# Row sums of an attention kernel: pair tiles joined by adding transfers, straight turns, another tile order

## The reference

```
xn  = layernorm(x)
x  += attention(xn) + experts(xn)
# attention, for each batch entry and head:
S   = q @ k.T * 32 ** -0.5            # 2048 x 2048
P   = exp(S - max(S)) / sum(exp(S - max(S)))
out = (P @ v) @ proj_w.T + proj_b
```

## Time and profile before

| | us |
|---|---|
| profiled execution | 5082.81 |
| its span on the core | 5081.0 |
| median of three runs | 5081.68 |
| TensorE busy | 4905.3 (97%) |
| TensorE weight loads | 2978.3 (59%) |
| VectorE busy | 3225.3 (63%) |
| ScalarE busy | 2454.4 (48%) |
| GpSimd busy | 3283.1 (65%) |
| mean granted TensorE clock | 0.983 of full speed |

### The profile page before, as it was taken

One profiled execution on the slowest core, in us unless ns is written; L12 is line 12 of the kernel. 1 busy time (PEld: TensorE's weight loads), 2 busy tenths in 40 slices (PEclk: granted clock), 3 DMA queues, 4 the chain that ended last, 5 costly groups with the idle time before them and its releaser, 6 DMA issues. The chain is left out here.

```text
span 5081.0 us, 84542 instructions
## 1 busy us (share of the span) xinstructions
PE 4905.3 (97%) x25932; PEld 2978.3 (59%) x25932; DVE 3225.3 (63%) x5424; ACT 2454.4 (48%) x4653; POOL 3283.1 (65%) x925
## 2 busy tenths in 40 slices
PE   8999999999899999999999999999999999999979
PEld 6878878878555555545554554555455455555447
DVE  4232333232577877777777777777777777778624
ACT  2121121121166666656665666666566566666631
POOL 1212211211288888888888888888888888888830
PEclk9999999999799999999999999999999999999989
DMA  5352433433311111211211211211211111121056
GB/s 171 93 156 87 131 112 117 123 116 118 89 30 49 46 41 48 47 43 43 51 37 43 57 35 44 53 41 39 53 46 35 49 48 41 41 53 30 14 177 236
DMA packets 217465, 366.39 MB, mean 72 GB/s; under 512 B 41156, under 2 KB 74948, under 8 KB 208840
## 3 DMA queue, kind: packets, MB, share of 16 engines
q1 hardware_dynamic: 217032, 360.85, 25.5%
HBM read 224.96 MB, written 134.74 MB: 71 GB/s over the span
## 5 line engine op out<-in xcount | busy, mean ns | idle before, releaser
L848 POOL TENSOR_TENSOR p_pair<-p_sb 128x2048 f32<-128x2048 f32 x512 | 2338.0, 4588 | 523.2 <-PE mx_ps L998 442.7
L903 DVE TENSOR_REDUCE unit_max<-mx_ps 128x1 f32<-128x512 f32 x4096 | 2512.0, 681 | 217.7 <-PE mx_ps L978 210.3
L889 ACT ACTIVATE p_sb<-st_ps 128x512 f32<-128x512 f32 x4096 | 2110.4, 616 | 1083.6 <-PE st_ps L1044 1074.3
L978 PE MATMUL mx_ps<-k_x,q_x 96*128 96x512 f32 x4096 | 1700.1, 419 | 71.8 <-DVE unit_max L903 52.1
L1044 PE MATMUL st_ps<-q_x,k_x 97*128 97x512 f32 x4096 | 1626.5, 410 | 19.5 <-issue 16.8
L978 PEld LDWEIGHTS mx_ps<-k_x,q_x 96*128 96x128 f32 x4096 | 784.1, 192 | 619.6 <-DVE unit_max L903 256.4
L990 PE MATMUL o_ps<-p_sb,v_sb 128*32 128x512 f32 x8192 | 996.9, 605 | 5.1 <-ACT p_sb L889 5.1
L1044 PEld LDWEIGHTS st_ps<-q_x,k_x 97*128 97x128 f32 x4096 | 774.6, 189 | 352.9 <-ACT p_sb L889 151.3
L285 POOL TENSOR_TENSOR h_lo<-h_f,h_hi 128x512 fp32r<-128x512 f32 x128 | 165.4, 1293 | 691.6 <-DVE h_hi L469 691.6
L838 POOL TENSOR_TENSOR p_pair<-p_pair 128x2048 f32<-128x2048 f32 x128 | 586.9, 4585 | 10.0
L990 PEld LDWEIGHTS o_ps<-p_sb,v_sb 128*32 128x32 f32 x8192 | 214.9, 109 | 504.0 <-ACT p_sb L889 298.7
(11 more groups left out here) (93 smaller groups left out, 3755.8 us busy)
## 6 DMA issues: line engine op xcount, KB each, us to landing
q_x<-q_hi_d SPq DMA_DIRECT2D x128, 256.0 KB, 7.2
k_x<-k_hi_d SPq DMA_DIRECT2D x68, 256.0 KB, 4.1
xt<-x SPq DMA_DIRECT2D x64, 256.0 KB, 2.7
stage<-w SPq DMA_DIRECT2D x32, 512.0 KB, 5.1
q_hi_d<-qk_hi SPq DMA_DIRECT2D x64, 256.0 KB, 3.0
q_lo_d<-qk_lo SPq DMA_DIRECT2D x64, 256.0 KB, 3.8
k_hi_d<-qk_hi SPq DMA_DIRECT2D x64, 256.0 KB, 2.6
k_lo_d<-qk_lo SPq DMA_DIRECT2D x64, 256.0 KB, 3.3
```

Source lines behind the costliest of these rows:

```text
L848: pool.tensor_tensor(p_pair[:, slot, :, :], p_sb[:, 2 * i % SLOTS, :, :], p_sb[:, (2 * i + 1) % SLOTS, :, :], ALU.add).then_inc(pair_done, 1)
L889: act.activation(p_sb[:, kt % SLOTS, h, :], st_ps[bank(g, m)][:, :], ACT.Exp, scale=SCALE).then_inc(exp_done, 1)
L903: dve.reduce_max(unit_max[:, n // 4, n % 4:n % 4 + 1], mx_ps[UNIT_PLACE[n] % RING][:, :], AX.X).then_inc(bank_read, 1)
L978: pe.matmul(mx_ps[UNIT_PLACE[n] % RING][:, :], q_x[qc][0:R, h, t * P:(t + 1) * P], k_x[u][0:R, h, kc * 512:(kc + 1) * 512], start=True, st ...
```

## The change

- Each pair's two tiles are added by GpSimd as before, but into four p_pair slots whose roles a, b, c, d rotate from group to group (pair_slots). Four times a group GpSimd issues an adding transfer (join): a whole 1 MB pair slot is added to another inside SBUF. One more add on GpSimd joins the last pair. So GpSimd does 9 adds a group instead of 10.
- There are three row-sum parts instead of six: slot a after two joins (in step 7), slot d after four joins (in step 2 of the next group), slot a again after GpSimd's last add (in step 3 of the next group). Slot a holds pairs 0, 1 and 2 at first; d holds pairs 3, 4 and 5; and a holds 6 and 7 at the end.
- p_sb has 7 slots instead of 8, filled by the tile's number in the whole run modulo 7.
- All turns are straight code on all engines.
- The order of tiles in the steps is another; T stands behind V alone, and a wait for its bank is added. A group has 68 places.

```diff
-    SLOTS = 8
+    SLOTS = 7
-    ADDS = [(0, 0, -1), (1, 1, -3), ("four", 1, None), (2, 0, None), (3, 2, -2), ("four", 2, None),
-            (4, 0, None), (5, 1, 0), (6, 2, 1), (7, 0, 2)]
-    PARTS = [(3, 1, 4), (6, 2, 6), (7, 0, 7), (8, 1, 7), (9, 2, 8), (10, 0, 9)]
+    def pair_slots(group):
+        a, b, c, d = 0, 1, 2, 3
+        for _ in range(group):
+            a, b, c, d = c, b, d, a
+        return a, b, c, d
+    NA, NJ = NP + 1, 4
+    PARTS = [(2, 0, False, 7), (4, 0, True, 10), (0, NA, False, 11)]
...
-        p_pair = sb("p_pair", [P, 3, 4, TOK], F32)
+        p_pair = sb("p_pair", [P, 4, 4, TOK], F32)
...
-        STEPS = ["SUSSUVZUSUSUSUSUSU", "SUSSUVZUSUSUSUSUSU", "SUSSUVUSUSUSUSUSU", "SUSSUVUSUSUSUSUSU",
-                 "SUSSUVZUSUSUSUSUSU", "SUSSUVUSUSUSUSUSU", "SUSSUVZTUSUSUSUSUSU", "SUSSUVZUSUSUSUSUSU"]
+        STEPS = ["USUSUSUVUSSUSUSUS", "USUSUSUVUSSUSUSUS", "USUSUSUVZUSSUSUSUS", "USUSUSUVZUSSUSUSUS",
+                 "USUSUSUVUSSUSUSUS", "USUSUSUVUSSUSUSUS", "USUSUSUVTUSSUSUSUS", "USUSUSUVZUSSUSUSUS"]
...
-                with sp.Fori(1, TURNS - 1) as L:
+                for L in range(1, TURNS - 1):
...
+                def join(into, slot):
+                    pool.dma_start(p_pair[:, into, :, :], p_pair[:, slot, :, :], accum_op=ALU.add).then_inc(joined, 16)
+                def group(at):
+                    a, b, c, d = pair_slots(at)
+                    if at > 0:
+                        pool.wait_ge(joined, at * NJ * 16)
+                    pair(at, 0, a)
+                    pool.wait_ge(pair_done, at * NA)
+                    pair(at, 1, b)
+                    pool.wait_ge(pair_done, at * NA + 2)
+                    join(a, b)
+                    if at > 0:
+                        pool.wait_ge(sum_done, at * NS - 1)
+                    pair(at, 2, c)
+                    if at > 0:
+                        pool.wait_ge(sum_done, at * NS)
+                    pair(at, 3, d)
+                    pool.wait_ge(pair_done, at * NA + 3)
+                    pool.wait_ge(joined, (at * NJ + 1) * 16)
+                    join(a, c)
+                    pair(at, 4, b)
+                    pool.wait_ge(pair_done, at * NA + 5)
+                    pool.wait_ge(joined, (at * NJ + 2) * 16)
+                    join(d, b)
+                    pair(at, 5, c)
+                    pool.wait_ge(sum_done, at * NS + 1)
+                    pair(at, 6, a)
+                    pool.wait_ge(pair_done, at * NA + 6)
+                    pool.wait_ge(joined, (at * NJ + 3) * 16)
+                    join(d, c)
+                    if at > 0:
+                        normalise(at)
+                    pair(at, 7, b)
+                    pool.wait_ge(pair_done, at * NA + NP)
+                    pool.tensor_tensor(p_pair[:, a, :, :], p_pair[:, a, :, :], p_pair[:, b, :, :], ALU.add).then_inc(pair_done, 1)
...
-                                act.activation(p_sb[:, kt % SLOTS, h, :], st_ps[bank(g, m)][:, :], ACT.Exp,
+                                act.activation(p_sb[:, (L * G * KT + n) % SLOTS, h, :], st_ps[bank(g, m)][:, :], ACT.Exp,
...
-                    adds, slot, at = PARTS[i]
-                    pe.wait_ge(pair_done, L * G * NA + g * NA + adds)
+                    joins, adds, in_d, at = PARTS[i]
+                    slot = pair_slots(L * G + g)[3 if in_d else 0]
+                    if joins:
+                        pe.wait_ge(joined, ((L * G + g) * NJ + joins) * 16)
+                    else:
+                        pe.wait_ge(pair_done, (L * G + g) * NA + adds)
...
                         elif step == "T":
+                            emptied(0, -1, TURNED, True, False)
                             turn_rows(1)
```

More of the change, by code:

```diff
@@ L590, in attention_stage @@
     RING = 4
-    ADDS = [(0, 0, -1), (1, 1, -3), ("four", 1, None), (2, 0, None), (3, 2, -2), ("four", 2, None),
-            (4, 0, None), (5, 1, 0), (6, 2, 1), (7, 0, 2)]
-    PARTS = [(3, 1, 4), (6, 2, 6), (7, 0, 7), (8, 1, 7), (9, 2, 8), (10, 0, 9)]
-    PAIR_ADDED = [[pair for pair, _, _ in ADDS].index(i) + 1 for i in range(NP)]
-    NA, NS = len(ADDS), len(PARTS)
-    NORM = 9
+    def pair_slots(group):
[5 more added lines that the diff above has]
+    PARTS = [(2, 0, False, 7), (4, 0, True, 10), (0, NA, False, 11)]
+    NS = len(PARTS)
     ctx = ExitStack()
@@ L645, in attention_stage @@
         SK = 4 * KT
[L650 to L651 removed]
+        STEPS = ["USUSUSUVUSSUSUSUS", "USUSUSUVUSSUSUSUS", "USUSUSUVZUSSUSUSUS", "USUSUSUVZUSSUSUSUS",
+                 "USUSUSUVUSSUSUSUS", "USUSUSUVUSSUSUSUS", "USUSUSUVTUSSUSUSUS", "USUSUSUVZUSSUSUSUS"]
         FIRST = sum(s.count("U") for s in STEPS[AHEAD:])
+        PARTS_AT = [at for _, _, _, at in PARTS]
         FILLS = [(j, i, step) for j in range(NP) for i, step in enumerate(STEPS[j]) if step in "UTZ"]
@@ L665, in filled @@
                 return not (last and g + (2 if j >= AHEAD else 1) >= G) and (g > -2 or j >= AHEAD)
-            return step == "Z" and not (first and (g < 0 or g == 0 and j < 2))
+            return step == "Z" and not (first and (g < 0 or g == 0 and j + NP in PARTS_AT))
         def reads(g, place, first, last):
@@ L688, in attention_stage @@
         PART_PLACE = {at: PLACE[at % NP, STEPS[at % NP].index("Z")] for at in PARTS_AT}
-        PARTS_ON = {at: sum(at == x for _, _, x in PARTS) for at in PARTS_AT}
-        PARTS_BY = {at: sum(x <= at for _, _, x in PARTS) for at in PARTS_AT}
+        PARTS_BY = {at: n + 1 for n, at in enumerate(PARTS_AT)}
         ALL_READS = read_count(TURNS - 1, G - 1, PLACES, False, True)
@@ L828, in normalise @@
                     pool.tensor_tensor(o_inv[:, :], o_raw[:, :], o_inv[:, :], ALU.mult).then_inc(o_done, 1)
[L830 to L849, removed]
@@ L851, in _, with pair @@
-                turn(0, True)
-                with pool.Fori(1, TURNS) as L:
-                    turn(L, False)
+                def pair(at, i, slot):
+                    pool.wait_ge(exp_done, at * SK + 8 * i + 8)
+                    n = at * KT + 2 * i
+                    pool.tensor_tensor(p_pair[:, slot, :, :], p_sb[:, n % SLOTS, :, :], p_sb[:, (n + 1) % SLOTS, :, :],
+                                       ALU.add).then_inc(pair_done, 1)
+                def join(into, slot):
+                    pool.dma_start(p_pair[:, into, :, :], p_pair[:, slot, :, :], accum_op=ALU.add).then_inc(joined, 16)
@@ L854, in _ @@
+                for at in range(NQ * QC):
+                    group(at)
                 normalise(NQ * QC)
@@ L887, in turn @@
                                     old = n - SLOTS
-                                    act.wait_ge(pair_done, since(L * G * NA, old // KT * NA + PAIR_ADDED[old % KT // 2]))
-                                act.activation(p_sb[:, kt % SLOTS, h, :], st_ps[bank(g, m)][:, :], ACT.Exp,
+                                    act.wait_ge(pair_done, since(L * G * NA, old // KT * NA + old % KT // 2 + 1))
+                                act.activation(p_sb[:, (L * G * KT + n) % SLOTS, h, :], st_ps[bank(g, m)][:, :], ACT.Exp,
                                                scale=SCALE).then_inc(exp_done, 1)
                 turn(0, True, False)
-                with act.Fori(1, TURNS - 1) as L:
+                for L in range(1, TURNS - 1):
                     turn(L, False, False)
@@ L958, in _ @@
                 turn(0, True, False)
-                with dve.Fori(1, TURNS - 1) as L:
+                for L in range(1, TURNS - 1):
                     turn(L, False, False)
@@ L1068, in sum_parts @@
                                 pe.wait_ge(shift_done, L * G + G)
-                            for i, (_, _, at) in enumerate(PARTS):
+                            for i, (_, _, _, at) in enumerate(PARTS):
                                 if at == (j if mine else j + NP):
@@ L1083, in turn @@
                                 elif not (last and g == G - 1):
+                                    emptied(L, g, TURNED, first, last)
                                     turn_rows(L * G + g + 2)
                 turn(0, True, False)
-                with pe.Fori(1, TURNS - 1) as L:
+                for L in range(1, TURNS - 1):
                     turn(L, False, False)
@@ L1093, in _ @@
                 for i in range(NS):
-                    if PARTS[i][2] >= NP:
-                        sums(TURNS - 1, G - 1, i, PART_PLACE[PARTS[i][2]])
+                    if PARTS[i][3] >= NP:
+                        sums(TURNS - 1, G - 1, i, PART_PLACE[PARTS[i][3]])
 def output_stage(nc, proj_wT, o_d, y_d, out):
```

7 lines of the change are left out of this document (3 added, 4 removed).

## The result

The changed kernel takes 4842.35 us (median of 4 runs, 4836.55 to 4845.29) against 5081.59: ratio 0.9526, interval 0.951 to 0.9543. The profiled execution took 4836.55 us, its span is 4834.7. The forecast was 4875.

A forecast was written before the change was run, and what follows sets the result against it. TensorE's own work (97% busy) was taken as the bound, GpSimd 6 us from it. From 5082.8 us, 62 x (54.52 - 51.1) = 212 off and 4.6 on for the tail gave 4875 us; own range 4820 to 4945 (0.49).

The forecast's parts named there:

- Straight turns: Attention stage's 48 looped intervals: written straight they take 53.26 us each, 79 us off in all.
- Places: Ring of four banks: 68 places instead of 70 padded to 72 remove TensorE's 0.95 us wait before step 0.
- Parts: TensorE's row sums: three parts a group fewer, 0.87 us each, 2.6 us off.
- i: GpSimd's time to issue one adding transfer: 1.1 us taken, ends 0.43 and 1.72.
- l: Adding transfer's time from issue to landing: 7.9 us (2.5 fixed, two reads of 2.7), ends 5.2 and 10.6.
- The path over pair 6: Step 7's part, pair 6, join 4's issue, multiply, copy, exponential, step 0's seventh score: TensorE stands 1.1 us a group.
- GpSimd's own sum: GpSimd per group: 42.6 us work, four issues of 1.1, 3.3 landing wait, 0.4 gaps: 50.7 us.
- two loops that meet once a group seldom mesh: TensorE's and GpSimd's cycles both come out near 50.8 us a group, so 51.1 us is taken.
- A: Rival, GpSimd's waits on landings: joins land late, GpSimd is the bound; slower, 5199 us, up to 5353; chance 0.22.
- C: Rival, GpSimd's issues: dearer joins at 1.72 us each, still faster, 5006 us; chance 0.20 together with the late-small-DMA rival.
- B: Rival, GpSimd's joins: cheap issues (0.43 us), quick landings (5.2 us), 4790 us; chance 0.07 for below 4820.
- D: Rival: a small DMA late, 1 to 3 us a group, 4937 to 5061 us; chance 0.20 together with dearer joins.

## Why the prediction was right, point by point

- **Straight turns**: 79 us forecast, 80 measured (5084.1 - 5003.6), half from the jumps and half from every step of the loop. **Places**: 59 forecast, 56 measured. **Tile order**: nothing, and nothing. **Parts**: 0.87 us each, and TensorE alone at 49.7 us: the kernel with multiply and loads moved comes to 49.8.
- **GpSimd's adds** stay at 4.6 us beside the transfers; the page's 4.81 contains overlaps with the issues' records.
- **i**, the length of a join's issue: 1.1 taken. From an issue's start to the end of one add behind it is 5.80 us at 1659.92, of which the first 0.34 lay under the add before: 0.9 us. **l**, from issue to landing: 7.9 taken, 7.3 by the page; the wait for join 2 is 2.0 to 2.4 us instead of 3.3, so 6.6 to 7.0 us after the end of its issue. That is near the sum of 2.5 us and two reads of 2.7, but the sum is not shown by it: for half a slot it would give 5.2 us, and the halves land after 6.4, two of them in flight together.
- **The path over pair 6** was found where it was placed: the seventh score of step 0, released by an exponential, 0.79 us a group against i = 1.1. It is the one wait that the change leaves on TensorE.
- **Mis-sized**: GpSimd's own sum. It was put at 50.7 us, level with TensorE's; by the kernel with three quarters of an add more it is 48.3 (50.6 less 2.3). Four issues shorter by 0.2 us and a wait shorter by about 1.2 make up most of that. So only one loop is near the bound, and the charge for "two loops that meet once a group seldom mesh", +0.3 us, was for nothing: GpSimd stands 2 us before pair 6, which the prediction did not have, and absorbs the variation. With i, this makes 51.1 instead of 50.61: 30 us. All of these missed to the same side; the forecast was 33 us too long by the medians and did not live on errors that cancel.
- **Left out**: the groups ahead of the first multiply gain too; counting 62 intervals of 64 groups lost 5 to 6 us, and the stage began 3.4 us earlier in this execution by chance. The tail, +5.0, was put at +4.6. 4875 - 30 - 9 = 4836, the profiled time, which was the lowest of the four.
- **Rivals.** A (joins land late and GpSimd is the bound) needed 54.5 us a group; GpSimd is at work for 46.3 us and waits 4.3. The kernel with adds on GpSimd shows what lies there. C's dear joins did not come: an issue took 0.9 us, not 1.72. B's landings of 5.2 us did not either. D (a small transfer is late): they do land 4 us later, and the 8 us of room for each held.

## What to carry to other kernels

Price a skipped slot of a ring and the jump of a hardware loop before the heavy work: together they were 136 of 240 us here. The first stood in the trace of before as one odd wait a group. The loop stood there as one odd interval in eight, and for its other half as 0.12 us more in every step, which only a comparison of looped with straight groups shows. A queue instruction that takes 0.9 us must not stand between a result and the engine that waits for it; put it behind, and then look at which transfers it meets there. And a wait of TensorE's that grows may cost more than its length: in the kernel with split transfers and in that with three quarters of an add more, about half of the groups ran on at a lower clock behind it, and others, with waits as long, did not.

## What had not been expected of the hardware

An adding transfer of 1 MB inside SBUF lands after 7.3 us at the median, beside some 48 GB/s of other transfers (131 GB/s less four joins of 1 MB in 50.6 us), and takes 0.9 us of GpSimd's time; with half the bytes it still takes about as long to issue (two in 1.77 us) and lands after 6.4 us. Issued 0.5 us ahead of SyncE's loads (2.25 MB in the group shown), it landed after 12.5 us. A transfer of 8 KB from SyncE's queue takes 5.9 us to land beside the joins and took 1.8 without them. And the clock may fall behind a wait of TensorE's of 1.46 us, and may stay behind one of 2.1 us.
